# A graph convolution on one core: who fetches the 416 tiles of source rows, and how the sums are cleared

## The reference

```
h   = relu(layernorm(x))
xs  = h_s @ W1_s / 8 ;  xv = h_v @ W1_v / sqrt(32)         # per node: the table
w   = silu(edge_embed @ fc_w1 + fc_b1) @ fc_w2 + fc_b2     # per edge: 192 weights
msg = w * (xs, xv)[src] * edge_sh                          # per edge: 384 products
agg = segment_sum(msg, dst) / sqrt(AVG_DEG)                # per node
out = x + h + gate(agg @ W2 + h @ Wsc)                     # per node, silu gates
```

## Time and profile before

| | |
|---|---|
| median of three runs | 542.44 us |
| lowest, highest | 542.05, 542.9 us |
| span of the profiled execution | 824.7 us |
| PE busy | 575.1 us, 70% of the span |
| POOL busy | 393.7 us, 48% |
| DVE busy | 354.3 us, 43% |
| ACT busy | 201.8 us, 24% |
| mean granted TensorE clock | 0.772 |

### The profile page before, as it was taken

The page is one execution under the profiler, slowest core; times in us unless marked ns, Lnnn a source line. Parts: engine busy times, 40 slices in busy tenths (PEclk is TensorE's granted clock), DMA queues, the critical chain, the costliest instruction groups (busy, mean ns, idle before and its releaser), DMA issues.

```text
span 824.7 us, 17164 instructions
## 1 busy us (share of the span) xinstructions
PE 575.1 (70%) x5423; PEld 415.1 (50%) x5423; DVE 354.3 (43%) x1234; ACT 201.8 (24%) x416; POOL 393.7 (48%) x425
## 2 busy tenths in 40 slices
PE   4175478678768678657775877687778558668767
PEld 3163355455446446445553654465456446556556
DVE  6163144343435444343443444353444444444345
ACT  2171221122213122221322222132223122222222
POOL 7507464554553455445444545544563455453340
PEclk8596586686797779779778866976797788886679
DMA  9632121111121112111111111111121111121110
GB/s 278 206 99 70 38 61 42 49 48 48 46 55 35 50 51 53 45 49 47 46 47 50 51 48 52 51 44 46 53 56 38 50 51 52 47 55 34 39 44 12
DMA packets 36230, 48.19 MB, mean 58 GB/s; under 512 B 10200, under 2 KB 28859, under 8 KB 35683
## 3 DMA queue, kind: packets, MB, share of 16 engines
q0 software_dynamic: 19776, 33.78, 15.1%
q1 hardware_dynamic: 16009, 13.98, 5.9%
q10 hardware_dynamic: 410, 0.07, 0.1%
HBM read 39.60 MB, written 4.00 MB: 53 GB/s over the span
## 4 chain that ended last, share of the span: by engine, by line
PE 38%; another core or an unknown queue 23%; DVE 14%; issue 12%; DVEq 4%; ACT 0%
PE ps L865 12%; PE ps L875 8%; PE ps L852 5%; DVE P L685 5%; PE ps L870 4%; DVE agg L723 4%; DVEq L708 2%; PE ps L871 2%; DVE P L680 2%; PE ps L907 2%; DVE M L665 1%; DVEq L723 1%; PE ps L858 1%; PE ps L900 1%
## 5 line engine op out<-in xcount | busy, mean ns | idle before, releaser
L567 POOL DMA_INDIRECT gath<-table,src_sb x388 | 367.4, 947 | 397.2 <-DVE P L685 272.3
L870 PE MATMUL ps<-S,P 128*64 128x36 f32 x832 | 135.2, 255 | 136.9 <-DVE agg L723 126.4
L875 PE MATMUL ps<-S,P 128*64 128x24 f32 x2496 | 206.4, 236 | 29.6 <-issue 29.5
L865 PE MATMUL ps<-fc_sb,hid 128*128 128x384 f32 x416 | 199.9, 601 | 14.7 <-issue 14.5
L875 PEld LDWEIGHTS ps<-S,P 128*64 128x64 f32 x2496 | 191.8, 163 | 28.4 <-issue 28.4
L870 PEld LDWEIGHTS ps<-S,P 128*64 128x64 f32 x832 | 94.4, 158 | 206.3 <-DVE agg L723 139.4
L600 ACT ACTIVATE hid<-ps,fb_sb 128x256 f32<-128x256 f32 x104 | 49.2, 473 | 459.9 <-remote 227.6
L680 DVE TENSOR_TENSOR P<-ps,gath 128x512 f32<-128x512 f32 x103 | 71.1, 690 | 162.3 <-PE ps L865 105.7
L865 PEld LDWEIGHTS ps<-fc_sb,hid 128*128 128x128 f32 x416 | 93.8, 238 | 71.1 <-issue 52.0
L871 PE MATMUL ps<-S,P 128*64 128x12 f32 x832 | 120.8, 222 | 9.7 <-issue 9.7
L665 DVE TENSOR_TENSOR M<-iota,dstrel 128x48 f32<-128x48 f32 x104 | 21.5, 207 | 236.7 <-remote 175.8
(11 more groups left out here) (119 smaller groups left out, 377.0 us busy)
## 6 DMA issues: line engine op xcount, KB each, us to landing
slow<-table SPq DMA_DIRECT2D x512, 0.6 KB
gath<-table,src_sb POOLq DMA_INDIRECT x388, 2.5
agg<-zeros SPq DMA_DIRECT2D x4, 1024.0 KB
out<-res SPq DMA_DIRECT2D x24, 78.1 KB
x_sb<-x SPq DMA_DIRECT2D x5, 350.0 KB
emb<-emb_t SPq DMA_DIRECT2D x104, 16.0 KB
table<-prod SPq DMA_DIRECT2D x3, 420.0 KB
sh_sb<-sh_t SPq DMA_DIRECT2D x1, 840.0 KB
```

Of the source, the lines that this page charges most:

```text
L567: nc.gpsimd.indirect_dma_start(gath[:, u, j, :], None, table, bass.IndirectOffsetOnAxis(ap=src_sb[:, t:t + 1], axis=0)).then_inc(arrived, 16)
L865: ins = nc.tensor.matmul(w_ps(u)[:, 2 * g:2 * g + 2, 0:WN], hid[:, u % 2, g, :], fc2_sb[:, :, :], start=False, stop=True, skip_group_check ...
L870: nc.tensor.matmul(oj[0:64, :, 0:3], pj[:, 64:128], sj[:, :, 1:4], start=True, stop=True)
L875: ins = nc.tensor.matmul(oj[64:128, :, c:4:3 - c], pj[:, lo:lo + 64], sj[:, :, 0:2 + c:1 + c], start=(c == 0), stop=(c == NC - 1), skip_gr ...
```

## The change

All 416 tiles are fetched from `table` by POOL in the loop. The tile `raw`, its statistics, its normalisation, transposes, matmuls and copies are gone; the 512 row fetches of SP with their register loads and the four copies of ACT are gone; so are `src_q` as an input, and the unrolled last four rounds on ACT and DVE (ACT's loop now runs to the last round, DVE's to the one before it). POOL clears columns 0 to 8191 of `agg` itself by one memset in place of `zeros` and the four DMAs.

```diff
-                for m in range(NS):
-                    t = (SLOW_FROM + m) * SLOTS * QT + 2 * QT - 1
-                    sp.dma_start(slow_i[:, m * TE:m * TE + TE], src_q[t:t + 1, :]).then_inc(s_slow, 16)
...
-                sp.wait_ge(s_agg, 1)
-                for lo in range(0, ZERO_DMA, ZEROS):
-                    sp.dma_start(agg[:, lo:lo + ZEROS], zeros[:, :]).then_inc(s_clear, 16)
...
-                nc.gpsimd.memset(zeros[:, :], 0.0).then_inc(s_agg, 1)
+                nc.gpsimd.memset(agg[:, 0:POOL_CLEAR], 0.0).then_inc(s_agg, 1)
                 pool.wait_ge(s_src, 16)
-                for r in range(NR):
-                    t = (RAW_FROM + r) * SLOTS * QT + SLOTS * QT - 1
-                    nc.gpsimd.indirect_dma_start(
-                        raw[:, r, :], None, x,
-                        bass.IndirectOffsetOnAxis(ap=src_sb[:, t:t + 1], axis=0)).then_inc(s_raw[r // RG], 16)
                 pool.wait_ge(s_iota, 2)
                 pool.wait_ge(s_agg, 1)
-                pool.wait_ge(s_clear, 16 * (ZERO_DMA // ZEROS))
...
-                clear(ZERO_DMA, (N + WIN) * AC)
-                for g in range(HEAD_RAW):
-                    raw_std(g)
+                clear(POOL_CLEAR, (N + WIN) * AC)
...
-                raw_moments(0)
                 windows()
-                raw_moments(1)
                 passes_needed()
                 output_weights()
-                for g in range(HEAD_RAW):
-                    raw_scale(g)
-                dve.wait_ge(s_rinv, HEAD_RAW)
...
-                            if i == 1 and u == 0:
-                                sp.wait_ge(s_slow, 16 * NS)
-                                sp.wait_ge(s_tabw, TABLE_IN)
-                            n0 = ROWS * ((i * SLOTS + u - SLOTS) // 2)
-                            if 0 <= n0 < NS * TE:
-                                if u % 2 == 0:
-                                    idx = indices(n0)
-                                    rows(n0, idx[0:ROWS // 2])
-                                else:
-                                    rows(n0 + ROWS // 2, idx[ROWS // 2:])
...
-                        raw_tile = u == SLOTS - 1 and q // SLOTS >= RAW_FROM
-                        slow_tile = u == 1 and q // SLOTS >= SLOW_FROM
-                        for j in range(QT - raw_tile - slow_tile):
+                        for j in range(QT):
...
-                        if with_raw and u == 1:
-                            ins = nc.scalar.copy(hrT[:, :, :], rawT_ps)
-                        if with_raw and u == 2:
-
-                            act.wait_ge(p_prod, q - 2)
-                            ins = nc.scalar.copy(gath[:, SLOTS - 1, QT - 1, :], raw_ps)
...
-                        if with_raw and u == 1:
-                            nc.tensor.transpose(rawT_ps[0:S0, 0, :], hr[:, 0:S0], ident[:, :])
-                            ins = nc.tensor.transpose(rawT_ps[:, 1, :], hr[:, S0:D], ident[:, :])
-                        if with_raw and u == 2:
-                            nc.tensor.matmul(raw_ps[:, 0:S0], hrT[0:S0, 0, :], w_s[0:S0, 0:S0], start=True, stop=True)
-                            ins = nc.tensor.matmul(raw_ps[:, S0:D], hrT[:, 1, :], w_tab[:, 0:VD], start=True, stop=True)
```

More of the change, by code:

```diff
@@ L33 @@
 EPS = 1e-5
-ZEROS, ZERO_DMA = 2048, 8192
 WARM_NODES = 17
@@ L37, with build @@
 PC = 320
[L40 to L49, removed]
+POOL_CLEAR = 8192
 assert NI * SLOTS == NQ and NN * NTN == N and NG * G == NN and NI - LEAD == NN - 2
-def build(nc, x, src_t, src_q, dst_t, dst_q, sh_t, emb_t, w1s, w1v, fc1, fb1, fc2, fb2, w2s, w2v, wscs, wscv, out):
+def build(nc, x, src_t, dst_t, dst_q, sh_t, emb_t, w1s, w1v, fc1, fb1, fc2, fb2, w2s, w2v, wscs, wscv, out):
     ctx = ExitStack()
@@ L146, in build @@
         s_x = [sem(f"s_x{g}") for g in range(NG)]
-        s_raw = [sem(f"s_raw{g}") for g in range(NR // RG)]
-        s_slow, s_src, s_rstat, s_rmv, s_rstd2, s_rinv = (sem("s_" + n) for n in ("slow", "src", "rstat", "rmv", "rstd2", "rinv"))
+        s_src = sem("s_src")
         s_idx, s_dq, s_wn, s_wo, s_oz = (sem("s_" + n) for n in ("idx", "dq", "wn", "wo", "oz"))
-        s_pz, s_ident, s_iota, s_agg, s_zero, s_clear, s_cact = (
-            sem("s_" + n) for n in ("pz", "ident", "iota", "agg", "zero", "clear", "cact"))
+        s_pz, s_ident, s_iota, s_agg, s_zero, s_cact = (
+            sem("s_" + n) for n in ("pz", "ident", "iota", "agg", "zero", "cact"))
         s_stat, s_std, s_rstd, s_z, s_hT, s_hTsb = (sem("s_" + n) for n in ("stat", "std", "rstd", "z", "hT", "hTsb"))
@@ L344, in output_weights @@
                         nc.vector.tensor_scalar_mul(ap, ap, k)
[L346 to L359, removed]
                 def windows():
@@ L520, in store @@
                         sp.dma_start(out[bass.ds(t * NTN, NTN), :], res[of(t)][:, :]).then_inc(n_out, 16)
[L522 to L532, removed]
                     for i in range(NI):
@@ L571, in _ @@
                         pool.wait_ge(p_gath[u], landed(NI - 1 - u // (SLOTS - 1), u))
-                    for j in range(QT - 1):
+                    for j in range(QT):
                         pool.wait_ge(p_last[j], 16)
@@ L601, in step @@
                                                    bias=fb1_sb[:, 0:1])
-                        if isinstance(i, int) and i >= SLOW_FROM and u == 0:
-                            act.wait_ge(p_slow[i - SLOW_FROM], 16 * TE)
-                            act.wait_ge(p_prod, q - 2)
-                            ins = nc.scalar.copy(gath[:, 1, QT - 1, :], slow[:, i - SLOW_FROM, :])
-                        with_raw = not (isinstance(i, int) and i < RAW_FROM)
-                        if with_raw and u == 1:
-                            ins = nc.scalar.copy(hrT[:, :, :], rawT_ps)
-                        if with_raw and u == 2:
-                            act.wait_ge(p_prod, q - 2)
-                            ins = nc.scalar.copy(gath[:, SLOTS - 1, QT - 1, :], raw_ps)
                         ins.then_inc(p_hid, 1)
@@ L625, in step @@
                             node_tile(tile)
-                    def raw_std(g):
-                        act.wait_ge(p_rmv, g - HEAD_RAW + 1)
-                        sl = slice(g * RG, g * RG + RG)
-                        nc.scalar.activation(raw_rstd[:, sl], raw_mv[:, sl, 1], ACT.Sqrt,
-                                             bias=eps[:, 0:1]).then_inc(p_rstd, 1)
                     for i in range(LEAD + 1):
@@ L635, in _ @@
                             step(i, u, i - LEAD if i >= LEAD else None)
-                        if i == 0:
-                            for g in range(HEAD_RAW, NR // RG):
-                                raw_std(g)
-                    with act.Fori(LEAD + 1, SLOW_FROM) as i:
-                        for u in range(SLOTS):
-                            step(i, u, i - LEAD)
-                    for i in range(SLOW_FROM, NI):
+                    with act.Fori(LEAD + 1, NI) as i:
                         for u in range(SLOTS):
@@ L794, in step @@
                                 gated(tile)
-                        if u == 2 and not (isinstance(i, int) and (i < RAW_FROM - 1 or i == NI - 1)):
-                            if not (isinstance(i, int) and i < RAW_FROM):
-                                dve.wait_ge(p_hidps, q)
-                            raw_rows(i + 1)
                         if tile is not None:
@@ L825, in _ @@
                             step(i, u, i - LEAD if i >= LEAD else None)
-                            if i == 0 and u < NR // RG - HEAD_RAW:
-                                raw_moments(HEAD_RAW + u)
-                            if i == 1 and u < NR // RG - HEAD_RAW:
-                                raw_scale(HEAD_RAW + u)
-                    with dve.Fori(LEAD + 1, SLOW_FROM) as i:
+                    with dve.Fori(LEAD + 1, NI - 1) as i:
                         for u in range(SLOTS):
                             step(i, u, i - LEAD)
-                    for i in range(SLOW_FROM, NI):
-                        for u in range(SLOTS):
-                            step(i, u, i - LEAD)
+                    for u in range(SLOTS):
+                        step(NI - 1, u, NI - 1 - LEAD)
                     dve.wait_ge(p_agg, NT)
@@ L845, in hidden @@
                     def hidden(i, q, u):
-                        with_raw = not (isinstance(i, int) and i < RAW_FROM)
-                        if with_raw and u == 1:
-                            pe.wait_ge(p_rh, i - RAW_FROM + 1)
                         pe.wait_ge(p_emb[u], (i + 1) * 16)
```

57 lines of the change are left out of this document (3 added, 54 removed).

## The result

The changed kernel takes 575.24 us (median of four runs, 574.28 to 576.92) against 542.25 us (541.82 to 542.9) of the kernel before. The ratio is 1.0609 with a 95% interval of 1.0593 to 1.0625: 33.0 us slower. The forecast was 573.7 us.

What follows compares the result with a forecast made beforehand. POOL, issuing fetches every 1.25 us nearly without pause, was taken as the bound. 35.0 - 0.7 - 3 = +31.3 us on 542.4 gave 573.7 us; own range 567 to 580, widened over rivals to 556 to 581.

Steps and rivals of the forecast that it cites:

- 28 x 1.25 = +35.0 us: POOL's loop: 28 more fetches, one behind the other at a pitch of 1.25 us, add 35.0 us.
- The bound of 26.5 us without the gap: POOL's loop: lower bound, 28 x 0.947 us, if the 0.30 us gap between fetches were the profile's.
- The closure: Whole kernel before: setup 39, POOL's loop 485 and tail 11 us make 535, 7 us under the measured time.
- The two holes on ACT: Setup in the profile before: ACT idle for 11.6 and 10.8 us, PE and DVE too; taken out of the plain setup.
- the 282 us: Profiled span of 824.7 us against 542.44 us plain for the kernel before; the excess taken as added by the profile.
- The setup, -0.7 and -3 us: Setup: -0.7 us for square roots and reciprocals behind ACT's clearing, -3 us for the transfers that go.
- SP, 7.4 us a round, no bound: SP's queue: 22 row fetches and two index loads a round take 7.4 us; removing them gains 0.
- The tail, 0: End of kernel: last tile now fetched, not computed; between -0.5 and +0.5 us, taken as 0.
- A: Rival, loop: PE at a clock of 0.87 bounds plain runs, not POOL; time falls to 511 us; chance 0.08.
- B: Rival, loop: plain pitch of POOL's fetches is 1.20 us and POOL partly waits for PE; 557 us; chance 0.08.
- C: Rival, setup: holes are real in plain runs and the lost 6 MB close them, -20 us; about 557 us; chance 0.09.
- D: Rival, loop: PE's granted clock falls to 0.74, a round needs 20.9 us, +23 us; 597 us; chance 0.05.

Runs made afterwards that it cites:

- experiment 10: Kernel before with ACT's clearing of columns 8192 to 12547 moved from the end of the setup to its start: 542.04 us, ratio 0.9993.
- Experiments 1 and 2: 1: kernel before, SP's 512 row fetches replaced by four POOL fetches, 547.33 us. 2: changed kernel with SP's row fetches put back, 570.4 us.
- Experiments 5 to 8: Changed kernel with 391 fetches, 266 fetches, or 64-row fetches, and kernel before with ACT's clearing moved: 760.16, 607.67, 826.6, 835.89 us; kernel before there 839.15.
- experiment 7: Changed kernel with 64 rows in place of 128 in each fetch from round 1 on: 826.6 us, ratio 0.991.
- experiment 4: Changed kernel with zeros and its four transfers put back in place of the memset: 572.9 us, ratio 1.0582 to the kernel before.
- experiment 12: Kernel before with ACT's early clearing and 25 in place of 24 tiles from x rows, 387 loop fetches: 542.07 us, ratio 0.9995.
- 9: Changed kernel with two tiles each of slots 0, 1 and 2 not fetched from round 1 on, 266 fetches: 453.16 us, ratio 0.8351.
- run 52: Not a run number: part of "a run 52% too long", the profiled execution of the unchanged kernel before, span 824.7 us against 542.44 us without a profile.
- experiment 8: Kernel before with ACT's clearing moved to the start of the setup, on the slower chip: 835.89 us, ratio 0.997.

## Why the prediction was right

**The step that carries it, 28 x 1.25 = +35.0 us.** Right. From first to last fetch it is 519.8 us in the changed kernel and 485.3 us in the one of experiment 10, the difference 34.5 us. The bound of 26.5 us without the gap fails: the 0.30 us stand between the fetches in every profile here. Experiments 1 and 2 give 5.3 and 4.8 us for four fetches.

**The closure.** Right in its conclusion and off in its parts. I had setup 39, loop 485, tail 11 us. The kernel of experiment 10 shows 41.4, 485.3 and 14.5 us, which is its span of 541.2. The 7 us that I left unexplained were 2.4 us of setup, 3.5 us of tail and about 1 us by which the time exceeds the span, none of it waits of POOL. The two holes on ACT are not in its profile.

**What the 282 us were.** Wrong. I put them down to the profiler. Experiments 5 to 8 show a kernel before of 839 us in plain runs. The numbers survived because the pitch of POOL, the full-clock durations of PE and the length of single instructions are the same on both chips. The remark that SP's instructions stretch the profile fails by experiment 7, which has none of its rows and takes 826.6 us, and by 2, which has them all and takes 570.4.

**The setup, -0.7 and -3 us.** This term was off by 3 us and its mechanism was another. The first fetch moved from 41.41 to 40.68 us, -0.7 us in all. Larger terms cancel in it. Without the 24 fetches of x rows, and with zeros' transfers, it stands at 36.90 us, -4.5; the time says the same, 572.9 us being 30.7 over the kernel before and not 35.0. The memset gives back 2.2, and 1.6 are the difference between executions shown at experiment 4. I had put the memset at 0 because nothing on POOL waits behind it, and did not look at what it does to DVE beside it. I had put the 24 fetches at 0 too, since ACT seemed to end the setup; experiment 12 shows that one more of them puts the first fetch from the table off by 0.94 us. That the two errors have opposite signs is luck; it kept the whole within 3 us. With the scatter between executions these terms are good to 1 or 2 us.

**SP, 7.4 us a round, no bound.** The conclusion held, the size did not. SP needs 7.8 us of 9.4 (83%) for two groups in the kernel of experiment 10, from 300.57 to 308.33 us, twice what I had:

```profile
300.57 0.33 SPq L513 DMA_DIRECT2D emb<-emb_t  x1
303.57 1.91 SPq L529 DMA_DIRECT2D slow<-table  x5
305.53 0.33 SPq L513 DMA_DIRECT2D emb<-emb_t  x1
306.05 2.28 SPq L529 DMA_DIRECT2D slow<-table  x6
```

It was nearly as close to being the next bound as PE, which was busy for 91% of a stretch there.

**The tail, 0.** 13.9 against 14.5 us, -0.6, at the edge of the half microsecond that I gave it.

**The rivals.** A (PE bound) is refuted by 10, and 9 agrees. B (a pitch of 1.20) is refuted by the pitch. C (the holes close) does not apply to the measured times, since 10 has no holes to close. It is true of the chip of experiments 5 to 8, so my sign for it, a first fetch before 45 us in the changed profile, could not tell it from a profile taken on another chip. D (the clock falls) did not come: the granted clock did go from 0.97 to 0.93 in the same stretch, with PE at 82% in place of 91%, but a round of PE's work stays under POOL's 20 us and POOL waits for nobody. The Trainium skill's rule ("DMA: Bandwidth & Descriptors", Anatomy of one DMA — SWDGE (gpsimd) path) that many descriptors can be emitted before their cost shows does not hold for these fetches, whose 1.25 us stand one behind the other 416 times.

## What to carry to other kernels

Take the engine whose instructions follow each other at a constant pitch, multiply the pitch (start to start, not the duration) by the count, and see whether setup, count and tail close on the time measured without a profile; here that gave a change of 33 us within 2 us although the profile was of a run 52% too long. Compare the span of a profile with the plain time before reading its waits. When such an engine is the bound, each fetch that another engine does in its place saves the full pitch, as long as no other stage gets longer by it (in experiment 12 the setup did) and the helper's own pitch, again start to start with its index loads, stays under the round: SP was at 83%, and twice the rows cost 238 us. And an operation that nothing waits for may still cost, through the engine that works beside it.

## What the runs showed of the hardware

- An indirect fetch of 128 rows of 640 bytes holds POOL for 0.948 us and is followed by the next after 1.25 us; with 64 rows it is 0.90 and 1.20 us.
- A POOL memset of 128 x 8192 floats takes 6.9 us, and beside it a DVE multiply of 96 x 3 elements took 6.28 us in place of 1.15, ending with it. The setup behind it came 2.2 us later.
- SP issued single rows with a register address at 0.40 us each; the load of eleven indices from SBUF into registers took 2.46 us in the median.
- With the DMA engines' mean busy share at 1.02, PE was busy for 4.39 and DVE for 4.79 of 5 us on one chip (experiment 10), and for 0.71 and 1.67 us on another (experiment 8).
- On the chip of experiments 5 to 8 the same kernel took 839 us in place of 542, with waits of 7 to 10 us about once a round on ACT and DVE whose releaser the profile does not show.
